# Expert blocks: a fourth buffer for the gathered rows, weights asked for before rows, and part of the padding written earlier

## The reference

```
x   = layer_norm(src + attn, ln1_g, ln1_b)
idx = remainder(floor(x @ router_w + router_b), 4)      # the token's expert
for e in range(4):
    y = relu(x @ W1[e] + b1[e]) @ W2[e] + b2[e]         # 128 -> 512 -> 128
    ff_out += where(idx == e, y, 0)
out = layer_norm(x + ff_out, ln2_g, ln2_b) + residual
```

## Time and profile before

| | us |
|---|---|
| time, median of 3 runs (lowest to highest) | 1306.74 (1300.44 to 1307.12) |
| the profiled execution: its own time | 1302.08 |
| the profiled execution: its span | 1300.3 |
| PE / DVE / ACT / POOL busy over the span | 1086.2 / 992.3 / 790.4 / 539.1 |

### The profile page before, as it was taken

How to read it: one execution, slowest core, us unless ns; L and a number is a source line. 1 busy time by engine, 2 the same in 40 slices (tenths; PEclk the granted TensorE clock), 3 DMA queues, 4 the chain that set the end, 5 groups by cost and what they waited for, 6 DMA issues and landing times.

```text
span 1300.3 us, 20911 instructions
## 1 busy us (share of the span) xinstructions
PE 1086.2 (84%) x6007; PEld 403.5 (31%) x6007; DVE 992.3 (76%) x2429; ACT 790.4 (61%) x1670; POOL 539.1 (41%) x677
## 2 busy tenths in 40 slices
PE   4978887298998898998998898898998889778882
PEld 3745544022222122222222222222222224334431
DVE  7557775088999889999999999999898923655563
ACT  2422332114887788888887888888887885234331
POOL 6414432221143353453443443443543233645565
PEclk9567787556999999999999999999999999899896
DMA  5000000413413413423323324324324030554540
GB/s 153 7 0 1 0 0 0 97 33 68 99 47 72 99 44 83 96 54 83 95 56 80 93 58 84 87 58 84 92 53 102 7 116 17 192 180 126 150 123 13
DMA packets 101865, 94.27 MB, mean 72 GB/s; under 512 B 23101, under 2 KB 93182, under 8 KB 101768
## 3 DMA queue, kind: packets, MB, share of 16 engines
q1 hardware_dynamic: 94968, 80.19, 26.1%
q0 software_dynamic: 5504, 12.73, 2.8%
q10 hardware_dynamic: 1296, 0.20, 0.1%
HBM read 50.83 MB, written 42.92 MB: 72 GB/s over the span
## 4 chain that ended last, share of the span: by engine, by line
DVE 28%; PE 24%; POOL 14%; issue 10%; DMA 2%; SPq 2%; ACT 1%; POOLq 0%; ACTq 0%; DVEq 0%
DVE a_mx L1371 22%; PE ps_o L986 8%; PE ps_x L964 6%; POOL out L1522 5%; PE ps_s L971 3%; PE ps_m L929 2%; DMA ks<-stacks 2%; POOL a_qk L1212 1%; POOL a_parts L1221 1%; SPq L835 1%; PE ps_m L945 1%; POOL a_tnorm L1192 1%; POOL a_tnorm L1228 1%; POOL a_row L1225 1%; POOL a_tnorm L1217 1%
## 5 line engine op out<-in xcount | busy, mean ns | idle before, releaser
L1371 DVE TENSOR_REDUCE a_mx<-ps_x 128x1 f32<-128x512 f32 x1024 | 641.1, 682 | 86.6 <-PE ps_x L964 82.6
L1056 ACT ACTIVATE a_prob<-ps_s 128x512 f32<-128x512 f32 x1024 | 543.5, 604 | 87.6 <-PE ps_s L971 81.3
L964 PE MATMUL ps_x<-ks,a_qs 48*128 48x512 bf16 x1024 | 350.3, 405 | 73.9 <-DVE a_mx L1371 47.5
L971 PE MATMUL ps_s<-a_qs,ks 50*128 50x512 bf16 x1024 | 333.2, 391 | 21.2 <-ACT a_prob L1056 21.1
L986 PE MATMUL ps_o<-a_prob,vaug 128*32 128x512 f32 x2048 | 277.6, 614 | 0.0
L964 PEld LDWEIGHTS ps_x<-ks,a_qs 48*128 48x128 bf16 x1024 | 76.3, 95 | 395.7 <-DVE a_mx L1371 321.7
L1522 POOL DMA_INDIRECT out<-vaug,e_ids x76 | 84.6, 1113 | 21.7 <-issue 21.4
L971 PEld LDWEIGHTS ps_s<-a_qs,ks 50*128 50x128 bf16 x1024 | 74.3, 94 | 55.9 <-ACT a_prob L1056 52.8
L1145 POOL DMA_INDIRECT rows<-a_row,a_pos_i x64 | 64.3, 1005 | 58.0 <-DVE a_pos_i L1342 31.4
L1133 POOL CAST a_mx_parts<-a_mx 128x32 bf16<-128x32 f32 x32 | 6.6, 205 | 190.1 <-DVE a_mx L1371 190.1
L1155 POOL TENSOR_SCALAR a_vareps<-a_mv 128x4 f32<-128x4 f32 x16 | 3.2, 199 | 157.1 <-DVE a_mv L1281 157.1
(11 more groups left out here) (241 smaller groups left out, 1574.4 us busy)
## 6 DMA issues: line engine op xcount, KB each, us to landing
stacks<-a_parts SPq DMA_DIRECT2D x192, 128.0 KB, 2.4
a_qs<-stacks SPq DMA_DIRECT2D x64, 192.0 KB, 4.6
ks<-stacks SPq DMA_DIRECT2D x64, 192.0 KB, 5.0
x_tok<-rows SPq DMA_DIRECT2D x19, 520.0 KB, 3.9
rows<-a_prob SPq DMA_DIRECT2D x7, 520.0 KB, 5.3
a_qk<-in_L_ffn_W SPq DMA_DIRECT2D x13, 256.0 KB
a_z<-in_L_ffn_W SPq DMA_DIRECT2D x7, 256.0 KB
a_z_t<-in_L_ffn_W SPq DMA_DIRECT2D x6, 256.0 KB
```

The source lines that it names most:

```text
L964: pe.matmul(ps_x[:, bank(i + 1, n), :], qs[1 - r][own, pair, qt * P:(qt + 1) * P], ks[1 - r][own, pair, :], start=True, stop=True).then_in ...
L971: pe.matmul(ps_s[:, bank(i, n), :], ks[r][own, pair, kt * P:(kt + 1) * P], qs[r][own, pair, :], start=True, stop=True).then_inc(qk_mm, 1)
L1056: act.activation(prob[:, (s // 2) % RING, u % 4, :], ps_s[:, bank(i, u), :], ACT.Exp, scale=SCALE).then_inc(exp_done, EXP_STEP)
L1371: dve.tensor_reduce(mx[:, half, col:col + 1], ps_x[:, bank(i + 1, n), :], AX.X, ALU.max)\
```

## The change

- **Rows**: the ring of rows has 4 buffers (`ROWS`), block j uses j % 4, and its load waits for `result_done` of block j-4 in place of j-3. x_t, y_t and the hidden layer have 2 buffers in place of 3 (`PAIR`); weights, biases, results and ids keep 3.
- **Order on SP**: for each block, first the weights and biases, after a wait for `y_done` of block j-3; then the rows, after a wait for `result_done` of block j-4. Both table reads (`value_load`) stand ahead of their waits.
- **Padding**: the tile of padding moves to a part of `vg_t` that is dead by then, and POOL fills it in the attention step of the last sequence. SP writes the 3 blocks of padding that need no counts (`sp_pad_behind`) between the loads of block 1 and block 2, still during attention; the 4 behind the experts' rows (`sp_pad_ends`) stay ahead of block 6.
- **Loops**: every block is written out one by one on every engine; all waits are on constants.

```diff
             for j in range(ex.EARLY):
                 if j == 2:
+                    ex.sp_pad_behind(sp)
                     sp.wait_ge(pv_mm, (B - 1) * (SLOTS // 2))
-                if j == 2 * ex.RING:
+                if j == 6:
                     sp.wait_ge(scattered, 16 * T * B)
-                    ex.sp_pad(sp)
-                ex.sp_load(sp, j, j % ex.RING)
+                    ex.sp_pad_ends(sp)
+                ex.sp_load(sp, j)
...
                 if i == B - 1:
                     ex.pool_constants(pool)
+                    ex.pool_padding(pool)
...
             body(B + 1, (B + 1) % 2)
-            pool.wait_ge(pv_mm, B * (SLOTS // 2))
-            ex.pool_padding(pool)
-            ex.pool_block(pool, 2, 2)
-            ex.blocks(nc.gpsimd, lambda j, r, before: ex.pool_block(pool, j, r), ex.RING)
+            for j in range(2, ex.NB):
+                ex.pool_block(pool, j)
...
+    def sp_load(self, sp, j):
+        at, w, r = slice(j, j + 1), j % self.RING, j % self.ROWS
+        e = sp.value_load(self.table[0:1, 0, at], min_val=0, max_val=E - 1)
+        one = bass.ds(e, 1)
+        if j >= self.RING:
+            sp.wait_ge(self.y_done, j + 1 - self.RING)
+            sp.sem_inc(self.sp_passed, 1)
+        sp.dma_start(self.w1[w], ...).then_inc(self.weights_in[w], 16)
+        sp.dma_start(self.w2[w], ...).then_inc(self.weights_in[w], 16)
+        sp.dma_start(self.biases[w][:], ...).then_inc(self.weights_in[w], 16)
+        start = sp.value_load(self.table[0:1, 1, at], ...)
+        if j >= self.ROWS:
+            sp.wait_ge(self.result_done, j + 1 - self.ROWS)
+            sp.sem_inc(self.sp_passed, 1)
+        sp.dma_start(self.rows[r], ...).then_inc(self.rows_in[r], 16)
```

More of the change, by code:

```diff
@@ L1094, in _ @@
             steps(nc.scalar, body)
[L1095 to L1099, removed]
+            ex.act_middle(act, 0, (2, 3))
+            ex.act_end(act, 0)
+            for j in range(1, ex.NB):
+                ex.act_block(act, j)
         @block.gpsimd
@@ L1379, in _ @@
             ex.dve_late(dve)
-            ex.dve_block(dve, 2, 2, 0)
-            ex.blocks(nc.vector, lambda j, r, before: ex.dve_block(dve, j, r, before), ex.RING)
+            for j in range(2, ex.NB):
+                ex.dve_block(dve, j)
 class Experts:
@@ L1417, in __init__ @@
         wide = T * row_w
[L1418 to L1423, removed]
+        self.rows = [part(tokens, r * wide, wide).rearrange("p (t w) -> p t w", t=T) for r in range(ROWS)]
+        at = ROWS * wide
+        self.x_t = [part(tokens, at + r * block_w, block_w) for r in range(PAIR)]
+        at += PAIR * block_w
+        self.y_t = [part(tokens, at + r * block_w, block_w) for r in range(PAIR)]
+        at += PAIR * block_w
         self.r_in = part(tokens, at, T * D).rearrange("p (t d) -> p t d", t=T)
-        self.hid = [part(values, r * FT * block_w, FT * block_w).rearrange("p (f t) -> p f t", f=FT) for r in range(RING)]
-        self.tn = part(values, RING * FT * block_w, T * D).rearrange("p (t d) -> p t d", t=T)
+        self.hid = [part(values, r * FT * block_w, FT * block_w).rearrange("p (f t) -> p f t", f=FT) for r in range(PAIR)]
+        at = PAIR * FT * block_w
+        self.tn = part(values, at, T * D).rearrange("p (t d) -> p t d", t=T)
+        self.padding = part(values, at + T * D, wide).rearrange("p (t w) -> p t w", t=T)
         self.result = [part(vaug, r * T * D, T * D).rearrange("p (t d) -> p t d", t=T) for r in range(RING)]
-        self.padding = part(prob, 0, wide).rearrange("p (t w) -> p t w", t=T)
         self.w1 = w1
@@ L1458, in __init__ @@
         self.padded = sem("padded")
-        self.rows_in = [sem(f"rows_in{r}") for r in range(RING)]
+        self.rows_in = [sem(f"rows_in{r}") for r in range(ROWS)]
         self.weights_in = [sem(f"weights_in{r}") for r in range(RING)]
@@ L1483, in wait @@
             engine.wait_ge(semaphore, value)
[L1485 to L1493, removed]
     def bcast(self, ap):
@@ L1580, in pe_layer1, with pe_layer2 @@
             self.wait(pe, self.hid_done, (j - 1) * self.FT + f + 1)
-            pe.matmul(self.ps_f[f], self.w1[r][:, f * P:(f + 1) * P], self.x_t[r], start=True, stop=True)\
+            pe.matmul(self.ps_f[f], self.w1[w][:, f * P:(f + 1) * P], self.x_t[j % self.PAIR], start=True, stop=True)\
               .then_inc(self.hid_mm, 1)
-    def pe_layer2(self, pe, j, r, before):
+    def pe_layer2(self, pe, j):
         FT = self.FT
@@ L1597, in pe_back, with pe_block, act_inputs, act_middle @@
         for t in range(self.T):
[L1598 removed]
+            mm = pe.transpose(self.ps_b[:, t * P:(t + 1) * P], self.y_t[j % self.PAIR][:, t * P:(t + 1) * P], self.ident[:])
         mm.then_inc(self.back_mm, 1)
[L1601 to L1607, removed]
+    def pe_block(self, pe, j):
+        self.pe_layer1(pe, j, range(self.FT))
+        self.pe_back(pe, j - 1)
+        self.pe_layer2(pe, j)
+    def act_inputs(self, act, j):
         act.wait_ge(self.xt_mm, j + 1)
         self.wait(act, self.hid_mm, (j - 1) * self.FT)
[L1610 to L1612 removed]
+        act.activation(self.x_t[j % self.PAIR], self.ps_a, ACT.Copy).then_inc(self.xt_done, 1)
+    def act_middle(self, act, j, fs):
+        w = j % self.RING
         if fs[0] == 0:
[L1614 removed]
+            act.wait_ge(self.weights_in[w], 48 * (j // self.RING + 1))
         for f in fs:
```

105 lines of the change are left out of this document (53 added, 52 removed).

## The result

The changed kernel takes 1270.93 us (median of 5 runs, 1264.88 to 1273.82), the kernel before 1306.74 (5 runs, 1300.44 to 1312.8). The ratio is 0.9743, 95% interval 0.9709 to 0.9778: faster, by 2.6%. The forecast was 1270, range 1261 to 1286. Ratios are of executions within 1.5% of the fastest of their kernel in the same set; the profiled executions of e5 (1271.83 us) and e12 (1296.54 us) lie outside that and are read for the stage alone.

What follows compares the result with a forecast made beforehand. PE's waits for rows, from a ring of buffers with too little lead, and the half clock after them bound the stage. Gains of 24.0 and 10.0 us gave 1268.1 profiled or 1272.7 by median; forecast 1270, range 1261 to 1286.

Steps and rivals of the forecast that it cites:

- The sum: Whole kernel: 24.0 us from the steady blocks plus 10.0 at block 6 give 34.0 us gained.
- The steady stretch, 24.0 us: Experts' blocks from 7 on: 7.75 us a block in place of 9.93, 24.0 us gained.
- The slack of 5 us for rows: Steady blocks: rows land at 12 to 13 us, PE wants them at 17.7, so 5 us are left.
- Rival (b): Steady blocks: the stall only moves to another wait, only the padding's 10 us stay; 1297 us, chance 0.05.
- the ring of four: Row loads on SP: waiting for DVE's last step four blocks back, not three, ends steady row waits; 24.0 us gained.
- The half clock: PE after a stall for rows: runs at half clock, costing 1.75 us a block beyond the idle time.
- The start, 10.0 us at turn(6): PE's transposes of block 6's rows, behind four paddings: at 1136.5 us in place of 1146.49, 10.0 us gained.
- Padding in attention and POOL's fill at nothing: Attention: three padding DMAs moved there and POOL's 0.99 us tile filling near 1040 us cost nothing.
- Loops at nothing: Experts' stage, all engines: writing loops out saves register steps and branches, counted as nothing.
- rival (d): Experts' stage: fetching straight code stalls blocks 7 to 18, 3.5 us each; 1315 us, chance 0.04.
- Rival (a): Steady blocks: POOL or DVE becomes the bound, with scatters of 1.6 us; 13 us back, 1283 us, chance 0.14.
- Rival (c): Block 6: padding costs nothing more and its rows aren't held; 9 us better, 1261 us, chance 0.09.

Runs made afterwards that it cites:

- e5: Changed kernel with block 6's weights first, then two late paddings, its rows, two paddings; 179.0 us from block 0's row transposes to the end, 7.5 less than changed.
- e12: Changed kernel with three buffers of rows and rows asked for before weights; ratio 0.981 to the kernel before, 9.22 us a block.
- e9: Changed kernel run once more, unaltered, beside the padding splits; median 1273.98 us, ratio 0.982 to the kernel before.
- e7: Changed kernel with one extra DVE product in each block, result unused; 1.5 us longer, ratio 0.983 to the kernel before.
- e8: Changed kernel with two extra DVE products in each block, results unused; 9.6 us longer, ratio 0.992 to the kernel before.
- e1: Changed kernel with the ring of rows back at three buffers; 16.4 us longer, 8.92 us a block, ratio 0.987 to the kernel before.
- e2: Changed kernel, four buffers kept, with rows asked for before weights on SP; 2.1 us less to the end, ratio 0.971 to the kernel before.
- e11: Changed kernel with one late padding ahead of block 6's rows and three behind; median 1263.17 us, ratio 0.970 to the kernel before.
- e3: Kernel before with its hardware loops written out block by block, nothing else; ratio 0.998 to the kernel before, 9.93 us a block.
- e10: Second run of the changed kernel with late paddings split two ahead of block 6's rows, two behind; median 1262.28 us, ratio 0.974 to the kernel before.
- e6: Changed kernel with all four late paddings ahead of block 7 instead of block 6; 3.9 us less than changed, ratio 0.973 to the kernel before.

## Why the prediction was right, and where it was not

- **The sum.** 34.0 us were forecast, 34.3 measured from turn(0). The profiled execution itself is 37.2 us shorter (1302.08 to 1264.88), since its stage began 3.1 us earlier. That the median came within 1 us of 1270 is luck: between medians the same kernel gained 26.2 us in e9's set and 35.8 in the first. Why executions differ by up to 26 us ahead of turn(0) stays open.
- **The steady stretch, 24.0 us.** Forecast 7.75 us a block from turn(7) on; measured 7.74, a gain of 24.0 (109.24 to 85.19). The bound named next, PE, is the bound: 20.00 us busy of 20. DVE's spare 0.8 us are there, as e7 and e8 show from both sides. The slack of 5 us for rows is there too: 9.5 us from issue to use, less 4.0 of landing. Rival (b), that the stall moves to another wait, didn't come true: PE waits for nothing.
- **What the 24.0 us belong to** depends on the order in which the parts are added. Taken away last, from the changed kernel, the fourth buffer is worth 13.0. With three buffers the early read of the table and the paired buffers are worth 7.8 of the 11.0 that are left and weights first 3.2 (e12, e1), each from one profile and so known to about the 1.7 us that one stall more or less at half clock makes. With four buffers weights first adds nothing (e2), and a slack of over 5 us leaves nothing for an early read of 0.8 either; but that the fourth buffer alone, with the table read behind the wait, gives all 24.0 is worked out and not run. So the prediction's attribution to the ring of four isn't refuted. What it didn't see is that the small parts give 11.0 without the fourth buffer: SP issues 0.8 us sooner, and stalls that get shorter by about that much mostly stop costing the half clock.
- **The half clock, "9.50 - 7.75 = 1.75 us" for a stall.** It holds after most waits of 2.0 us and more. It does not hold after waits of 0.4 to 1.9 us (e1, e5, e11, e12), behind which the clock stayed at 1.00; the step of 8.20 behind the 1.84 us of e12 is longer by a wait for weights. And it is no fixed price: three waits of 2.6 to 2.7 us cost no clock at all, one each before, in e3 and in e12, with steps of 7.80 or 7.81 behind them. In the kernel before it is turn(10) (timeline of PE, then windows):

```profile
1186.38 0.66 PE L1572 MATMUL ps_x<-ident,x_tok 128*128 128x128 f32 x4 [2.69 <-DMA x_tok<-rows]
...
1194.18 0.60 PE L1572 MATMUL ps_x<-ident,x_tok 128*128 128x128 f32 x4
```

```profile
1186.00:1190.00 4.00, 3.62 (x12) 1.95 (x13) 3.07 (x7) 1.64 (x3) 3.39 (x3) 1.00 0.49 159
```

  The sum wasn't touched by this, since it went by the mean of 9.93 us. The step behind the long wait at turn(6) took 9.77 us, 10.81 in e9 and 9.24 in e7, where 9.50 was forecast.
- **The start, 10.0 us at turn(6).** Measured 10.4. The steps: turn(3) has no wait; the first padding's issue came 3.4 us after the last scatter's start, not 4.2; four paddings took 4.34 us, not 5.52; rows 6 took 5.4 us to PE, not 3.9. That they queue behind 512 KB of weights and paddings still draining fits e2, e5 and e11, where they took 4.6, 5.1 and 4.5. The issue came 2.0 us sooner than in the sum and the landing 1.5 us later; that these errors cancel is luck. The wait was forecast at about 7, and is 7.14.
- **Padding in attention and POOL's fill at nothing**: right; the rows of block 2, issued at 1065 behind them, are wanted at turn(2), 27 us later.
- **Loops at nothing**: right (e3, the same end within 0.1 us); rival (d), fetching of straight code, has no sign.
- **Rival (a)**: POOL's scatters stayed at 0.97 to 1.32 us with DVE busy 0.71 of the time, and with DVE busy 0.81 of it (e8, 1195 to 1235 us). By the Trainium skill's SBUF — State Buffer, section Who interferes with whom, closer packing could have held them; these runs show 1.33 us at the longest, against the 1.30 of the earlier trace rows.
- **Rival (c)**, that the padding costs nothing more, didn't come true in this change, but e5, e10 and e11 reach 5.0 to 7.5 us of its 9 (e10 against e9, the others against the changed kernel's first profile): it was a matter of where the paddings stand on SP.

## What to carry to other kernels

When a load waits for a buffer, count the lead in the bottleneck's own blocks, and put everything the load needs besides the buffer (here a table read of 0.8 us) ahead of the wait. With three buffers the early read (beside the paired buffers) gave 7.8 of the 24.0 us; the fourth buffer gave what was still missing and made the order of loads indifferent. Once no wait is left in the steady part, look at what stands in the queue ahead of the one wait that remains: paddings that nobody needed for three more blocks held block 6 for 7 us, and splitting them gave 5.0 to 7.5 us more.

## What the hardware showed that was not expected

- After waits of PE of 1.6 us or less the granted clock stayed at 1.00 (2.4 GHz) in e1, e5, e6 and e11. After 2.71 us in e10 it was 0.59 over the next 4 us, mostly the lower level (1.2 GHz); after 2.69 us in the kernel before it stayed at 1.00. So the length of the wait alone doesn't settle it here, and what else does isn't shown. Between e10 and e5 a wait shorter by 1.1 us gave 2.8 us.
- From 1134 to 1142 us of the kernel before, while the last of the seven paddings were issued and written, the DMA engines moved 410 GB/s:

```profile
1134.00:1142.00 8.00, 8.00 (x19) 3.44 (x17) 2.11 (x7) 3.44 (x5) 2.20 (x3) 0.82 1.03 410
```

  This is above the figure of about 358 GB/s for HBM that the prediction cites from the Trainium skill, DMA: Bandwidth & Descriptors, section Specifications. That row is half of what two cores share (716 GB/s by two), and here one core ran, so for a core by itself the measurement decides.
